# A GRU over time on one core: order of the first loads, the last part of W_hh in two transfers, and step 0's n in a PSUM bank of its own

## What is computed

```python
def reference(x, cond_2048, L1_cond_W_ih, L1_cond_W_hh, L1_cond_b_ih, L1_cond_b_hh):
    # x: (16, 256, 512)  cond_2048: (16, 512)  W_ih, W_hh: (512, 1536)
    x = x + _L0_cond_ref(x, cond_2048[:, None, :])     # causal depthwise filter over time, 16 taps
    x = x + _L1_cond_ref(cond_2048, x, W_ih, W_hh, b_ih, b_hh)
    return x

def cell(h, x):                                        # scanned over 256 steps, h starts as cond
    gi = x @ W_ih + b_ih
    gh = h @ W_hh + b_hh
    i_r, i_z, i_n = jnp.split(gi, 3, axis=-1)
    h_r, h_z, h_n = jnp.split(gh, 3, axis=-1)
    r = jax.nn.sigmoid(i_r + h_r)
    z = jax.nn.sigmoid(i_z + h_z)
    n = jnp.tanh(i_n + r * h_n)
    h_new = (1.0 - z) * n + z * h
    return (h_new, h_new)
```

## Time and profile before

| | us |
|---|---|
| median of 3 runs | 1027.0 (1026.89 to 1027.08) |
| the profiled execution | 1026.88 |
| its span, first to last instruction | 1025.1 |
| TensorE busy | 1014.5 (99%) |
| VectorE busy | 865.6 (84%) |
| ScalarE busy | 399.4 (39%) |
| GpSimd busy | 237.7 (23%) |
| step 0's first recurrent matmul | 17.7 |
| step 1's first recurrent matmul | 24.86 |

### The profile page before, as it was taken

The page is one execution under the profiler, slowest core; times in us unless marked ns, Lnnn a source line. Parts: engine busy times, 40 slices in busy tenths (PEclk is TensorE's granted clock), DMA queues, the critical chain, the costliest instruction groups (busy, mean ns, idle before and its releaser), DMA issues.

```text
span 1025.1 us, 58209 instructions
## 1 busy us (share of the span) xinstructions
PE 1014.5 (99%) x24837; PEld 935.8 (91%) x24838; DVE 865.6 (84%) x2850; ACT 399.4 (39%) x1816; POOL 237.7 (23%) x784
## 2 busy tenths in 40 slices
PE   8999999999999999999999999999999999999997
PEld 5987777777999999999999999999999999999996
DVE  7788888888888888888888898888888877777554
ACT  5334333343433334343333434333343433334342
POOL 3222222222222222222222222222222222222222
PEclk9999999999999999999999999999999999999999
DMA  8721000010100101001010010101001000000000
GB/s 296 73 34 39 19 21 30 15 36 19 31 23 15 32 19 34 24 11 35 15 39 19 15 36 11 39 19 29 26 11 35 14 29 18 9 29 4 25 14 12
DMA packets 66450, 32.07 MB, mean 31 GB/s; under 512 B 43920, under 2 KB 65040, under 8 KB 66192
## 3 DMA queue, kind: packets, MB, share of 16 engines
q1 hardware_dynamic: 65760, 28.25, 10.8%
q10 hardware_dynamic: 432, 0.11, 0.0%
HBM read 19.86 MB, written 8.49 MB: 28 GB/s over the span
## 4 chain that ended last, share of the span: by engine, by line
PE 97%; issue 2%; POOL 1%; DVE 0%; DMA 0%; ACT 0%; POOLq 0%; DVEq 0%
PE pg L307 65%; PE pg L297 32%; POOL tz L259 1%; PE pcv L335 0%; DMA cnd<-cond 0%; DVE hp L542 0%; DVE gn L521 0%; POOL nzh L272 0%; DVE gt L517 0%; POOLq L44 0%; POOL cpad L251 0%; ACT rz L439 0%; DVE an L529 0%; POOL cpad L249 0%; POOL nzh L256 0%
## 5 line engine op out<-in xcount | busy, mean ns | idle before, releaser
L307 PE MATMUL pg<-whh,hp 128*32 128x192 f32 x16368 | 717.8, 326 | 4.2 <-DVE hp L542 2.8
L307 PEld LDWEIGHTS pg<-whh,hp 128*32 128x32 f32 x16368 | 616.7, 110 | 53.9 <-issue 4.7
L297 PE MATMUL pg<-wih,x 128*32 128x192 f32 x8192 | 386.4, 326 | 0.0
L272 POOL TENSOR_TENSOR nzh<-rz,hp 128x32 f32<-128x32 f32 x512 | 158.1, 309 | 782.0 <-ACT rz L439 782.0
L297 PEld LDWEIGHTS pg<-wih,x 128*32 128x32 f32 x8192 | 307.5, 110 | 24.0
L439 ACT ACTIVATE rz<-gt 128x64 f32<-128x64 f32 x512 | 136.8, 267 | 484.6 <-DVE gt L517 460.8
L484 DVE SCALAR_TENSOR_TENSOR x<-xb,cnd,x 128x512 f32<-128x512 f32 (+1 forms) x420 | 295.1, 703 | 8.0
L542 DVE TENSOR_TENSOR_SCAN hp<-zcp,nzh 128x96 f32<-128x96 f32 x512 | 173.7, 339 | 41.8 <-ACT nzh L444 41.5
L517 DVE STREAM_TRANSPOSE gt<-pg 128x128 f32<-128x128 f32 x512 | 160.5, 314 | 50.6 <-PE pg L307 43.8
L529 DVE TENSOR_TENSOR_SCAN an<-rz,gn 128x64 f32<-128x64 f32 x512 | 149.2, 291 | 52.3 <-ACT rz L439 51.8
L444 ACT ACTIVATE nzh<-an 128x32 f32<-128x32 f32 x512 | 120.8, 236 | 126.8 <-DVE an L529 126.8
(11 more groups left out here) (45 smaller groups left out, 46.8 us busy)
## 6 DMA issues: line engine op xcount, KB each, us to landing
xb<-x SPq DMA_DIRECT2D x96, 94.0 KB, 2.0
out<-x SPq DMA_DIRECT2D x60, 128.0 KB, 1.9
wih<-w_ih SPq DMA_DIRECT2D x4, 768.0 KB, 7.9
whh<-w_hh SPq DMA_DIRECT2D x4, 768.0 KB, 14.5
xw<-x SPq DMA_DIRECT2D x24, 64.0 KB, 3.5
xb<-x SPq DMA_DIRECT2D x16, 62.0 KB, 1.9
tz<-taps SPq DMA_DIRECT2D x12, 64.0 KB, 3.4
xs<-x SPq DMA_DIRECT2D x1, 512.0 KB, 4.6
```

Source lines behind the costliest of these rows:

```text
L272: pool.tensor_tensor(nzh[:, f, ::2, :, 1], chunks(rz[:, f, 1, :, 1]), h_of(t - 1, slice(f * CH, (f + 1) * CH)), ALU.mult).then_inc(s_zh[f], 1)
L297: i = pe.matmul(pg[m % Q][f][D * j:D * (j + 1), RZ:END], x1_of(c, 2 * m, 2 * m + 2), wih[:, c, :, :].rearrange("p (g k) (j d) -> p j g k d ...
L307: i = pe.matmul(pg[t // 2 % Q][f][D * j:D * (j + 1), 0:IN], hp[:, t % 2, 2 * c + 1 - t % 2:2 * c + 3 - t % 2, :, 1].rearrange("p u b -> p ...
```

## The change

SP no longer issues cond; ScalarE does, ahead of the two biases. SP issues the last part of W_hh as two transfers, r and z first (`s_whh[3]`), n behind (`s_whl`). Step 0 is computed as `recur_rz` into the pair's bank and `recur_n` into `pcv[1]`, a bank that is free until step 6, for all four chunks; both read the landed parts, so TensorE doesn't wait for ScalarE's copies before step 1. `pcv[1]` is cleared by one more zero matmul and seeded by two more ScalarE instructions. Of the pair of steps 4 and 5, the product of chunk 3 comes first: half 0 behind chunk 0 of step 0, half 1 behind chunk 1; chunk 0 of half 0 comes behind chunk 2; chunks 1 and 2 after the last part. Step 1 has three products in place of four. The last of n signals `s_gn`, on which VectorE's `transpose_n(0, f)` waits. The constants LATE and IDLE change.

```diff
-LATE = 22
-IDLE = {0: 5, 1: 3}
+LATE = 18
+IDLE = {0: 3, 1: 4}
...
-            sp.dma_start(cnd[:, :, :], cond).then_inc(s_cnd, 16)
             sp.dma_start(xs[:, :, :], x[:, :, 0:TB * B]).then_inc(s_xs, 16)
             for c in range(C):
                 sp.dma_start(wih[:, c, :, :], w_ih[:, c, :, :]).then_inc(s_wih[c], 16)
-            for c in range(C):
+            for c in range(C - 1):
                 sp.dma_start(whh[:, c, F:], w_hh[:, c, :]).then_inc(s_whh[c], 16)
+            sp.dma_start(whh[:, C - 1, F:3 * F], w_hh[:, C - 1, 0:2 * F]).then_inc(s_whh[C - 1], 16)
+            sp.dma_start(whh[:, C - 1, 3 * F:], w_hh[:, C - 1, 2 * F:]).then_inc(s_whl, 16)
...
-            def product(m, f, c):
+            def product(m, f, c, last=C - 1):
...
+                if m == 2 and c == C - 1:
+                    pe.wait_ge(s_seed[f], m + 1)
...
-                if c == C - 1:
+                if c == last:
                     i.then_inc(s_gi[f], 1)
...
-            def recur_first(f, c):
+            def recur_rz(f, c):
+
                 for j in range(J):
+                    i = pe.matmul(pg[0][f][D * j:D * (j + 1), RZ:IN],
+                                  hp[:, 0, 2 * c + 1:2 * c + 3, :, 1].rearrange("p u b -> p (u b)"),
+                                  whh[:, c, F:3 * F].rearrange("p (g j f n) -> p j f g n", g=2, j=J, f=H)[:, j, f],
+                                  start=False, stop=True, skip_group_check=True)
+                return i
+
+            def recur_n(f, c):
+
+                for j in range(J):
+                    i = pe.matmul(pcv[1][D * j:D * (j + 1), f * RZ:(f + 1) * RZ],
+                                  hp[:, 0, 2 * c + 1:2 * c + 3, :, 1].rearrange("p u b -> p (u b)"),
                                   whh[:, c, 3 * F:].rearrange("p (j f n) -> p j f n", j=J, f=H)[:, j, f],
                                   start=False, stop=True, skip_group_check=True)
                 return i
...
+            pe.matmul(pcv[1][:, :], zeros[:, 0:P], zeros[:, :], start=True, stop=True).then_inc(s_bits, 1)
...
-            for c in range(C):
+            pe.wait_ge(s_seed_n, H)
+            for c in range(C - 1):
                 pe.wait_ge(s_whh[c], 16)
-                if c < C - 1:
-                    pe.wait_ge(s_whn, c + 1)
                 for f in range(H):
-                    if c < C - 1:
-                        recur(0, f, c)
-                    else:
-                        recur_first(f, c).then_inc(s_gh[f], 1)
+                    recur_rz(f, c)
+                    recur_n(f, c)
+                if c < H:
+                    product(2, c, C - 1, C - 2)
                 for _ in range(IDLE.get(c, 0)):
                     pe.matmul(pcv[0][:, :], zeros[:, 0:P], zeros[:, :], start=True, stop=True)
-            for c in range(C):
-                product(2, 0, c)
+            product(2, 0, 0, C - 2)
+            pe.wait_ge(s_whh[C - 1], 16)
+            for f in range(H):
+                recur_rz(f, C - 1).then_inc(s_gh[f], 1)
+            pe.wait_ge(s_whl, 16)
+            recur_n(0, C - 1)
+            recur_n(1, C - 1).then_inc(s_gn, 1)
+            for c in range(1, C - 1):
+                product(2, 0, c, C - 2)
...
-                    if m + 2 < M2:
-                        product(m + 2, t % 2, c)
+                    if m + 2 < M2 and not (t == 1 and c == C - 1):
+                        product(m + 2, t % 2, c, C - 2 if t == 1 else C - 1)
...
+            act.dma_start(cnd[:, :, :], cond).then_inc(s_cnd, 16)
             act.dma_start(bih[:, :], b_ih).then_inc(s_small, 16)
...
+            for f in range(H):
+                act.activation(pcv[1][:, f * RZ:(f + 1) * RZ], bc[:, f, 0:RZ], ACT.Copy).then_inc(s_seed_n, 1)
...
             for c in range(C):
-                act.wait_ge(s_whh[c], 16)
+                act.wait_ge(s_whh[c] if c < C - 1 else s_whl, 16)
                 act.activation(whh[:, c, 0:F], whh[:, c, 3 * F:], ACT.Copy).then_inc(s_whn, 1)
...
             def transpose_n(t, f):
+                if t == 0:
+                    dve.wait_ge(s_gn, 1)
+                g = pg[t // 2 % Q][f][:, 0:RZ] if t else pcv[1][:, f * RZ:(f + 1) * RZ]
                 dve.transpose(gn[:, t // 2 % 2, :, f, :, :, 0].rearrange("p u c b -> p c u b"),
-                              pg[t // 2 % Q][f][:, 0:RZ]).then_inc(s_tn[f], 1)
+                              g).then_inc(s_tn[f], 1)
```

## The result

The changed kernel takes 1032.2 us (median of 6 runs, 1031.6 to 1033.1), the kernel before in the same runs 1026.9: a ratio of 1.0051 (95% interval 1.0041 to 1.0061), 5.3 us slower. The forecast was 1026.2, within 1025.4 to 1027.1. The profiled execution took 1032.51 us with a span of 1030.8, 5.7 more than before.

The account below looks back on a forecast made before the run. TensorE, busy 99% of the span, was taken to bound the kernel. Step 1 starting 0.52 us earlier plus 0.20 saved in step 1 gave 0.72 off the 1027.0 median, 1026.28, stated as 1026.2; range 1025.4 to 1027.1.

Parts of the forecast that it names:

- The start: First loads on SP and ScalarE: x issued 0.45 us earlier, gain 0.0 to 0.45, taken as 0.45; later biases hidden.
- rival b: First loads: x comes no earlier because cond is in its way on another queue; gain 0.27 us, 1026.7; chance 0.17.
- The cover: VectorE before the filter: it waits for x until 5.38 us, hiding bias transposes that end at about 4.65.
- Rival (c): TensorE's clock falls to 1.2 GHz in the new idle microsecond before step 1, at 23.3 to 24.3: 1030; chance 0.03.
- TensorE's eight terms: Step 0 on TensorE: chunks, products, switches and filler bursts from 17.00 us to the last part's r and z at 21.99.
- step 1 to step 2 3.70: Step 1 has one product less, 0.325 us, of which only 0.20 is gained before VectorE's chain binds; bounds 0.10 to 0.325.
- the new wait for n: VectorE in step 0: n's transpose ends at 23.19, before the scan's 23.24, so the wait costs nothing by 0.05 us.
- The term of 0.66: Step 0's last part: 0.33 us half's issue plus 0.33 drain and semaphore; r and z alone take 0.22 plus 0.33.
- Rival (a): Step 0: TensorE is faster than summed and ScalarE's copy ahead of the sigmoid binds; gain 1.1 to 1.2, 1025.85; chance 0.27.

Follow-up runs that it names:

- the kernel with one small load: The changed kernel with cond and both biases as one transfer, issued first on ScalarE's queue: 1026.16 us, ratio 0.9992.
- the kernel with 17 more matmuls: The changed kernel with 17 matmuls on zeros after the products of steps 0 to 3, filling TensorE's wait for the transposes: 1030.45 us, ratio 1.0033.
- the kernel with LATE = 22: The kernel with one small load, with LATE set back from 18 to 22: 1026.24 us, ratio 0.9990.

## Why the prediction was wrong, step by step

- **The step that failed** is one sentence of "The start": b_hh leaves at 1.70, so the bias transposes end at about 4.65, and VectorE waits for x until 5.38 even so. It carried over the 1.7 us from issue to landing, a duration measured while the engines were free, to a moment at which W_ih's stream was there. The load took 6.4 us, 4.7 more than the sum had, and the bias transposes ended at 9.35 in place of 4.65. I asked what cond's neighbour on the queue costs cond and x (rival b), and not what cond costs the two behind it. The taps row on the same page (7.3 us) was the price in that state. (That row is a store of 96 KB, so as a price for 6 KB it is a bound and no more.) With it as the other bound, b_hh would have stood at 3.4 to 9.0 us, and the upper end would have put the filter at 10 us.
- **The cover** was named (VectorE waits for x anyway), but not what it costs if it is gone. The bias work is in VectorE's order ahead of the filter: 1.1 us of work and every microsecond of its wait then go straight to TensorE's start.
- **The loss in numbers.** Against the kernel with one small load, step 1 starts 6.42 us later. TensorE starts 20.89 - 16.87 = 4.02 later, and needs 7.39 - 4.98 = 2.41 more up to the last part. From there to step 1 both take the same (2.44 and 2.45). The first is VectorE's wait, the second the clock, confirmed by the kernel with 17 more matmuls.
- **Rival (c)**, the clock, had the right mechanism and the wrong place. I gave it 0.03 for the new idle microsecond before step 1. That microsecond did no harm (0.94 us idle, step 1's matmuls at full speed). The clock fell in the wait for VectorE, which the failed step had hidden. That its 1030 is nearer the measured 1032.2 than my forecast is luck. The chance of about 0.1 that I gave to all outside the range, "mostly (c)", does not follow from 0.03 for (c) and 0.03 for something unseen either.
- **Rival (b)** was wrong: x came 0.5 to 0.8 us sooner (first read at 5.06 to 5.35 us for 5.83), and not 0. The rule of the Trainium skill that the prediction cites (page "DMA: Bandwidth & Descriptors", section "Issuing engines are not separate DMA queues"), that issuing from a second engine saves only the sequencer's time, gives x's gain about rightly, though every trace shows a little more than the 0.45. It says nothing of what the two loads behind cond would pay: cond kept its 1.8 us, and b_hh lost 4.7.
- **The sum of the rest** stood, as the kernel with one small load shows: TensorE's eight terms 4.99 (4.98 measured), step 1 to step 2 3.70 (3.70). Two errors cancel: x was there 0.17 sooner than said, and the new wait for n, which I had at nothing, costs 0.2 (the transpose of n at 22.76, 0.44 after that of r and z, for 0.24 before). The term of 0.66 from TensorE's start on the last part to the first transpose, 0.55 for r and z alone, measured 0.47.
- **Rival (a)**, ScalarE's copy, is what comes next once TensorE is earlier, as the kernel with LATE = 22 shows.

## What to carry to other kernels

A small load's time from issue to landing holds only for the traffic in which it was measured. Before a load is moved one place down or started half a microsecond later, look at when the large stream begins, and count its packets against the stream's: each costs a turn. Look also at how late the first packet of another small transfer came in that traffic. Put small operands that gate an in-order engine into one transfer at the very start, and place the instruction that waits for them behind work that does not need them. And where the only thing that hid a delay is another wait, as ScalarE's copy did here, taking that wait out also takes out the cover.

## What the runs showed of the hardware that I had not expected

- A load of 6 KB took 1.7 us with only small rows of cond and b_ih beside it. It took 3.6 us when it was issued 0.48 us later behind a 32 KB load, or when x was issued 0.44 us earlier than before. It took 6.4 to 6.8 us with both.
- Idle time of TensorE does not tell alone whether its clock falls. It fell by the end of an idle 2.2 us in one run and 2.4 us into one in another, and held through 3.01 us in a third.
- Taking 32 KB off the head of SP's queue brought x 0.5 to 0.8 us sooner (5.06 to 5.35 for 5.83), for 0.45 us of issue. Each kernel has one trace, and kernels with the same first loads differ by up to 0.2 us, so how much there is beyond the issue is open.
- A small load can wait for its first packet with its own queue empty: 3.8 us for `taps` in the kernel before (issued at 3.33, first packet at 7.1).
